# Where the last stage's weights are prepared: rounding and moments moved into the attention, GpSimd given two experts, shares computed before the weights' rests

## The chip, the cores and the metric

The kernel runs on one core of a Trainium2 chip. The metric is the device time of one execution in microseconds (us). A difference under about 0.2% (3.4 us here) can't be told from no change by such measurements.

## The reference

Four stages run on a tensor `h` of 4 batches of 750 tokens of 192 numbers: a token mixer, an attention with a mixture of experts (8 experts, 2 per token), a windowed attention of 12 heads with relative positions, and a second mixture of experts (8 experts, 1 per token). The change concerns the end of the third and the start of the fourth.

```
h = h + _L1_attn_ref(_layernorm(h), ...)
# _L1_ffn_ref(_layernorm(h), Ws, bs, W1, b1, W2, b2), x = normalised tokens
logits = xt @ Ws + bs
probs = softmax(logits); routes = argmax(probs); prob_max = max(probs)
h1 = gelu(einsum('td,edf->etf', xt, W1) + b1)      # 192 -> 768, per expert
y = einsum('etf,efd->etd', h1, W2) + b2            # 768 -> 192
out = y[routes] * prob_max
h = h + out
```

## The kernel before

Tokens lie in 24 blocks of 125 (`NT`), six per batch. Each stage is a block in which every engine has its own program, written out by hand, with semaphores between them; a stage begins when all engines have left the one before.

The windowed attention works on a batch in two halves of six heads. A half is 36 "words" (head u, query block c, x = 6(u-u0)+c): TensorE computes `scores(x+1)`, a further block of row scores (until x = 27) and `values(x-1)`; ScalarE takes the exponential twice per word (`Phi` rounded to fp32r and `PT` in fp32); VectorE forms the rest `Plo = PT - Phi` and the row maxima. `exp(x)` waits for `values(x-2)`, since there are two buffers. After the last word come the relative tables, the division, and the projection, whose six blocks VectorE adds to `h` (`update(0)` to `update(5)`).

The last stage (`moe` with `gated` false) routes tokens. VectorE normalises all 24 blocks into `xn` (L1367), TensorE turns them and computes logits, VectorE adds the router's bias (`lg`, L1437), ScalarE takes the exponential (L1303), VectorE finds the maximum and the expert (`oh`, `msk`), TensorE ranks tokens (L1131), VectorE turns ranks into positions, one-hot tables (`tile0`, `tile1`, `lane1`), TensorE multiplies them to lists (L1145), VectorE makes the gather list `take` and the scatter list `give`, and GpSimd gathers rows of 128 tokens. The list of experts per tile is `eid` (`owners()`). A loop over 31 tiles of 128 tokens follows, at about 4.7 us a tile. `keep_running(n)` issues n multiplications of the identity that compute nothing of use (L1083; each shows as two instructions); they stand where TensorE would otherwise wait.

The first weights W1 (192 x 768 per expert) are used as a rounded part plus a rest, for which each expert has four slots. `round_weights(e)` makes three copies to fp32r on ScalarE (L1266 to L1268), and `rest_of_weights(e)` two subtractions on VectorE (L1352, L1354). Experts 0 and 1 are loaded during the attention (`LOADED`), the others at the start of the last stage. Before, expert 0 is rounded behind the last words (L2619 to L2621) and its rests formed before the updates (L2932, L2934); expert 1 is rounded among the turned tokens, expert 2 before the exponential, the others behind it; the rests of expert 2 stand behind `msk`, those of 3 to 7 behind `give`. `divided()` divides the largest exponential by the sum; `part`, `tileP` (L1570) and TensorE's `probabilities()` (L1174) bring that share into the tiles' order. The first tile's product needs all rests (`s_wl`), the loop needs the shares.

The moments of `h` (mean, variance of each token) for batches 0 to 2 are formed in the last words; those of batch 3 in the last stage, among the normalisations (L1399, L1405).

Of the kernel before, what the change touches and what calls it, by code (L numbers as in the profile page):

```python
# [12 lines left out]
F32 = mybir.dt.float32  # L13
# [744 lines left out]
SOON = 2  # L758

LOADED = 2  # L760
# [41 lines left out]
def moe(nc, keep, A, h, ident, cfg, out, st=None, w1=None, wr=None, row=None, room=None, share=None, Y=None,  # L802
# [4 lines left out]
    with ctx:  # L807
# [41 lines left out]
        known = st is not None  # L849
        if not known:  # L850
            st = sb("st", [P, NT, 6])
# [90 lines left out]

        s_w1 = {} if cfg.gated else {e: sem(f"w1_{e}") for e in range(LOADED, NE)}
        s_wb, s_wh, s_wl, s_xo = (None if cfg.gated else sem(k) for k in ("wb", "wh", "wl", "xo"))
# [44 lines left out]
        def _(pool):  # L989
# [51 lines left out]

            pool.wait_ge(s_X, stored)
# [35 lines left out]
        def _(pe):  # L1078

            def keep_running(n):  # L1080

                for _ in range(n):
                    nc.tensor.matmul(spare[:, 0:128], ident[:], ident[:], start=True, stop=True)  # L1083

            ahead_of = dict(zip(("tiles", "rank", "list", "sums", "gather", "second", "shares"),
                                (16, 26, 60, 3, 28, 12, 0) if cfg.gated else (6, 18, 44, 3, 26, 8, 12)))
# [69 lines left out]
            def first_products(buf, e, order=FIRST):  # L1156
                half = cfg.cols // 2
                for g in range(2):
                    for x, (m, k) in enumerate(order):
                        if order is ROUNDED_FIRST and k == 1 and g == 0:  # L1160
                            pe.wait_ge(s_wl, NE)
# [17 lines left out]
            for j in range(2):  # L1179
# [4 lines left out]
                to_columns(j)  # L1184
            pe.wait_ge(s_xc, 1)
# [3 lines left out]
            else:  # L1189
                pe.wait_ge(s_wbr, 32)  # L1190
                pe.wait_ge(s_wh, NE)
# [8 lines left out]
            if not cfg.gated:  # L1200
                keep_running(ahead_of["shares"])
                probabilities()
                pe.wait_ge(s_w, 16 * (NE + 1))
# [37 lines left out]
        def _(act):  # L1241
# [20 lines left out]
            def round_weights(e):  # L1262

                if e >= LOADED:
                    act.wait_ge(s_w1[e], 32)
# [14 lines left out]

            for t in range(NT):
# [6 lines left out]
                else:  # L1288
                    if t == CH - 1:
                        act.wait_ge(s_wb, 16)  # L1290
                        nc.scalar.activation(bias_hi[:], bias_lo[:].bitcast(F32), ACT.Copy).then_inc(s_wb, 1)
                    if t % CH == CH - 1 and 0 < t // CH < SOON:
                        round_weights(t // CH)
                    if t == CH - 1:
                        roots(B - 1)

                        act.sem_inc(s_wh, 1)
                        nc.scalar.activation(warm[:], ident[0:1, 0:1], ACT.Exp)
            logits_out(NT // GROUP - 1)
            if not cfg.gated:  # L1300
                round_weights(SOON)
# [3 lines left out]
            if not cfg.gated:  # L1305
                for e in range(SOON + 1, NE):
                    round_weights(e)
# [38 lines left out]
        def _(dve):  # L1346
# [3 lines left out]
            def rest_of_weights(e):  # L1350
                dve.wait_ge(s_wh, e + 1)
# [44 lines left out]
            else:  # L1396
                def statistics(b):
# [1644 lines left out]
```

## Time and profile before

| | us |
|---|---|
| median of 3 runs | 1686.12 |
| lowest, highest | 1685.95, 1686.94 |
| profiled execution, its own time | 1683.9 |
| its span | 1682.0 |
| TensorE busy | 1586.4 (94%) |
| VectorE busy | 1172.5 (70%) |
| ScalarE busy | 983.9 (58%) |
| GpSimd busy | 415.2 (25%) |

The profiled execution took 1.9 us more than its span and 2.2 us less than the median of the runs. The attention's last half runs from about 1356 us (first exponential) to 1468.5 us (last update), the last stage's preparation from 1469.1 to 1525 us, and its loop to the end. Times of the rows are us from the span's start.

### The profile page before, as it was taken

How to read it: one execution, taken by the hardware profiler on the slowest of the kernel's cores; microseconds unless marked ns; L12 is line 12 of the kernel's file. 1: busy time of each engine (PE TensorE's matmuls, PEld its weight loads, DVE VectorE, ACT ScalarE, POOL GpSimd, SP SyncE). 2: the span in 40 equal slices, each digit the busy share in tenths (PEclk: the TensorE clock that was granted, in tenths of full speed). 3: DMA queues.
4: the chain of work that ended last, by engine and by line, in shares of the span. 5: the costliest groups of instructions: out<-in, count | busy, mean ns of one | idle time of the engine just before them, and what ended most of it. 6: DMA issues, size and time to landing. Idle time of an engine off the chain costs nothing. (4 is left out here: it accounts for less than half of the span.)

```text
span 1682.0 us, 32345 instructions
## 1 busy us (share of the span) xinstructions
PE 1586.4 (94%) x11573; PEld 1460.9 (87%) x11574; DVE 1172.5 (70%) x2224; ACT 983.9 (58%) x1775; POOL 415.2 (25%) x583
## 2 busy tenths in 40 slices
PE   5999999988999999999999999999999999889997
PEld 5788999977899888889898889888889988878996
DVE  4887555548776786786787677677677688575443
ACT  5542222225778678678677668767767857562331
POOL 4131566650102101210200310310300300014443
PEclk9999999988999999999999999999999999999999
DMA  9212111155101100100110110110110111091111
GB/s 271 72 47 85 52 56 58 56 131 142 45 11 40 45 11 24 61 11 11 44 40 10 30 46 20 30 46 20 30 46 11 39 50 38 23 299 52 60 59 29
DMA packets 61923, 94.73 MB, mean 56 GB/s; under 512 B 15644, under 2 KB 46511, under 8 KB 61422
## 3 DMA queue, kind: packets, MB, share of 16 engines
q1 hardware_dynamic: 52606, 72.92, 14.9%
q0 software_dynamic: 9200, 20.21, 4.2%
q8 instruction: 79, 1.29, 0.3%
q14 instruction: 38, 0.31, 0.1%
HBM read 72.58 MB, written 21.06 MB: 56 GB/s over the span
## 5 line engine op out<-in xcount | busy, mean ns | idle before, releaser
L2771 DVE TENSOR_REDUCE a_nmx<-a_M 125x1 f32<-125x752 f32 x256 | 240.6, 940 | 125.5 <-PE a_M L2239 125.0
L2593 ACT ACTIVATE a_Phi<-a_S 125x756 fp32r<-125x756 f32 x288 | 231.0, 802 | 159.3 <-PE a_O L2362 146.2
L2896 DVE TENSOR_TENSOR a_Plo<-a_PT,a_Phi 125x756 fp32r<-125x756 f32 x288 | 281.7, 978 | 51.7 <-ACT a_PT L2593 50.8
L2593 ACT ACTIVATE a_PT<-a_S 125x756 f32<-125x756 f32 x288 | 229.9, 798 | 0.0
L1989 POOL TENSOR_TENSOR a_qlo<-a_work,a_qhi 127x750 fp32r<-127x750 f32 x48 | 79.2, 1659 | 565.8 <-PE a_S L2343 494.7
L2343 PE MATMUL a_S<-a_qhi,a_khi 128*125 128x378 f32 x576 | 154.8, 350 | 10.5 <-issue 6.6
L2355 PE MATMUL a_O<-a_Phi,a_vhi 125*128 125x378 f32 x576 | 150.1, 342 | 1.3 <-ACT a_PT L2593 1.3
L2362 PE MATMUL a_O<-a_Plo,a_vhi 125*128 125x378 f32 x576 | 147.5, 337 | 1.0 <-DVE a_Plo L2896 0.9
L2343 PE MATMUL a_S<-a_qlo,a_khi 128*125 128x378 f32 x576 | 146.8, 336 | 0.0
L2343 PE MATMUL a_S<-a_qhi,a_klo 128*125 128x378 f32 x576 | 146.7, 336 | 0.0
L2358 PE MATMUL a_O<-a_Phi,a_vlo 125*64 125x378 f32 x576 | 146.4, 335 | 0.0
L1231 PE MATMUL m_psY<-m_w,m_hidT 128*128 x696 | 130.0, 330 | 2.8 <-DVE m_hidT L1588 2.8
L2239 PE MATMUL a_M<-a_khi,a_qhi 127*125 127x376 f32 x512 | 132.2, 339 | 0.2 <-DVE a_nmx L2771 0.2
L1231 PEld LDWEIGHTS m_psY<-m_w,m_hidT 128*128 128x128 f32 x696 | 114.4, 189 | 9.7 <-issue 9.7
L2343 PEld LDWEIGHTS a_S<-a_qhi,a_khi 128*125 128x125 f32 x576 | 98.4, 187 | 23.0 <-issue 15.9
L2362 PEld LDWEIGHTS a_O<-a_Plo,a_vhi 125*128 125x128 f32 x576 | 104.1, 189 | 14.5 <-DVE a_Plo L2896 4.3
L1315 ACT ACTIVATE m_xT<-m_psX 128x128 fp32r<-128x128 f32 x85 | 23.6, 277 | 153.1 <-PE m_psX L1153 153.1
L2355 PEld LDWEIGHTS a_O<-a_Phi,a_vhi 125*128 125x128 f32 x576 | 101.9, 190 | 11.2 <-issue 8.2
L1165 PE MATMUL m_psG<-m_w,m_xT 128*128 x540 | 109.2, 348 | 0.7 <-issue 0.6
L2015 POOL COPY a_by_column<-a_pairs 128x540 f32<-128x540 f32 x21 | 28.3, 1346 | 324.2 <-ACT a_pairs L2473 176.7
L2343 PEld LDWEIGHTS a_S<-a_qhi,a_klo 128*125 128x125 f32 x576 | 103.8, 187 | 0.0
L2343 PEld LDWEIGHTS a_S<-a_qlo,a_khi 128*125 128x125 f32 x576 | 103.7, 187 | 0.0
(463 smaller groups left out, 3273.1 us busy)
## 6 DMA issues: line engine op xcount, KB each, us to landing
a_qhi<-a_rdens SPq DMA_DIRECT2D x48, 187.5 KB, 3.3
a_wkv<-a_w4k SPq DMA_DIRECT2D x8, 768.0 KB, 5.2
a_wq<-a_w4q SPq DMA_DIRECT2D x8, 768.0 KB, 6.7
a_wkv<-a_w4v SPq DMA_DIRECT2D x8, 768.0 KB, 5.5
m_w<-in_m_w SPq DMA_DIRECT2D x8, 576.0 KB, 9.1
m_X<-m_xn SPq DMA_DIRECT2D x8, 504.0 KB
m_w<-in_m_w SPq DMA_DIRECT2D x8, 384.0 KB, 9.4
m_w_ahead<-in_m_w SPq DMA_DIRECT2D x8, 384.0 KB, 8.3
```

What stands on the lines that cost most here:

```text
L1165: last = nc.tensor.matmul(psG[buf][:, g, 0:half], tokens, w1[0:rows_, bass.ds(e, 1), k, g * half:(g + 1) * half].rearrange("d o f -> d (o ...
L1231: last = nc.tensor.matmul(psY[:, 0:E], hidT[:, k * 128:(k + 1) * 128], w2[:, bass.ds(here, 1), k, :].rearrange("f o e -> f (o e)"), start= ...
L1989: pool.tensor_tensor(qlo[0:ONE, u % HG % QLO, :], work[0:ONE, u % HG, 0:L], qhi[0:ONE, u % HG, :].bitcast(F32), ALU.subtract).then_inc(sg[ ...
L2015: pool.tensor_copy(to[:, pr, :, 0:GRID], rows[:, pr, 0:FULL, :])
L2239: last = nc.tensor.matmul(bank[0:P, a, 0:376], qhi[0:ONE, u % HG, c * P:(c + 1) * P], khi[0:ONE, u % HG, a * 374:a * 374 + 376], start=Tru ...
L2343: last = nc.tensor.matmul(psS[wd % 2][0:P, a, 0:HP], kk[:, u % HG, at], qq[:, PART[a]:PART[a] + HP], start=(x == 0), stop=(x == 2))
L2355: nc.tensor.matmul(psO[:, a, 0:HP], vhi[:, c, u % HG, :], Phi[:, wd % 2, at[a]], start=(c == 0), stop=False)
L2358: nc.tensor.matmul(psO[0:HD, a, 0:HP], vlo[:, c, u % HG, :], Phi[:, wd % 2, at[a]], start=False, stop=False)
L2362: last = nc.tensor.matmul(psO[:, a, 0:HP], vhi[:, c, u % HG, :], Plo[:, wd % 2, at[a]], start=False, stop=(c == CH - 1))
L2593: last = nc.scalar.activation(to[:, wd % 2, :].rearrange("p (a l) -> p a l", a=2), psS[wd % 2][0:P, :, 0:HP], ACT.Exp, scale=SCALE)
L2771: v.tensor_reduce(nmx[:, u % 2, c:c + 1], bank[0:P, :, 0:376], AX.XY, ALU.max, negate=True).then_inc(sg["max_ready"], 1)
L2896: v.tensor_tensor(Plo[:, wd % 2, :], PT[:, wd % 2, :], Phi[:, wd % 2, :].bitcast(F32), ALU.subtract).then_inc(sg["exp_rest"], 1)
```

## The change

- Experts 0 and 1 are rounded by ScalarE in the last batch's second half, one of six copies ahead of the exponentials of words 14 to 19 (`next_weights`), and their rests are formed by VectorE behind words 28, 30, 33 and 34 (`next_rests`).
- In the tables' memory the order is changed, so that both experts' slots are free by then.
- The moments of batch 3 move to the end of the attention: four `bn_stats` ahead of `update(5)`, two and the six aggregations behind it.
- GpSimd rounds the bias and experts 2 and 3, in seven copies behind the stores of zeros; ScalarE rounds experts 4 to 7.
- VectorE forms the rests of expert 2 before it takes the logits. Behind `msk` it divides; `owners()` moves behind `give`; `part` and `tileP` come before the rests of experts 3 to 7.
- TensorE computes the shares between the turning of the first and the second gathered tile; 26 spare multiplications stand before the first tile's product.

In VectorE's program, the last words of the attention stand like this before (`a_Plo` is the rest of a word, the last row but one the copy of turned sums, then the last word's rest and its output):

```order
L2860 TENSOR_SCALAR late<-late 125x18
L2896 TENSOR_TENSOR a_Plo<-a_PT,a_Phi 125x756 x2
L2881 COPY a_work<-a_turning 32x756
L2896 TENSOR_TENSOR a_Plo<-a_PT,a_Phi 125x756
L2873 COPY a_work<-a_O 96x378
```

and like this now:

```order
L2886 TENSOR_SCALAR late<-late 125x18
L2922 TENSOR_TENSOR a_Plo<-a_PT,a_Phi 125x756
L2860 SCALAR_TENSOR_TENSOR m_w_ahead<-m_w_ahead 128x768
L2922 TENSOR_TENSOR a_Plo<-a_PT,a_Phi 125x756
L2907 COPY a_work<-a_turning 32x756
L2860 SCALAR_TENSOR_TENSOR m_w_ahead<-m_w_ahead 64x768
L2922 TENSOR_TENSOR a_Plo<-a_PT,a_Phi 125x756
L2899 COPY a_work<-a_O 96x378
```

Two subtractions of weights now stand between the rests of the last three words.

VectorE behind the scatter list `give`, before:

```order
L1535 CAST m_give<-m_who 128x31
L1352 SCALAR_TENSOR_TENSOR m_w_ahead<-m_w_ahead 128x768
...
L1360 TENSOR_TENSOR m_xT<-m_psX,m_xT 128x128
L1361 TENSOR_TENSOR m_xT<-m_psX,m_xT 64x128
L1364 COPY m_hres<-m_xg 128x192
L1538 TENSOR_REDUCE m_lm<-m_lg 125x24
...
L1570 TENSOR_TENSOR m_tileP<-m_tile,m_part 125x2232
L1620 COPY m_prob<-m_psY 128x31
```

and now:

```order
L1533 CAST m_give<-m_who 128x31
L1510 TENSOR_TENSOR m_ecmp<-m_iots,m_cum 1x264
...
L1555 TENSOR_TENSOR m_tileP<-m_tile,m_part 125x2232
L1362 SCALAR_TENSOR_TENSOR m_w_ahead<-m_w_ahead 128x768
...
L1364 SCALAR_TENSOR_TENSOR m_w_ahead<-m_w_ahead 64x768
L1370 TENSOR_TENSOR m_xT<-m_psX,m_xT 128x128
L1371 TENSOR_TENSOR m_xT<-m_psX,m_xT 64x128
L1374 COPY m_hres<-m_xg 128x192
L1610 COPY m_prob<-m_psY 128x31
```

The owners and the shares have moved ahead of the ten subtractions of experts 3 to 7; the second tile's rests come last instead of `tileP`.

GpSimd ahead of the first gather, now (before, the gather followed the stores of zeros):

```order
L1022 DMA m_Y<-m_zero 128x192 x4
L1053 CAST m_bias_hi<-m_bias_lo 8x768
L1045 CAST m_w_ahead<-m_w_ahead 128x768
L1047 CAST m_w_ahead<-m_w_ahead 64x768
L1049 CAST m_w_ahead<-m_w_ahead 64x768
L1045 CAST m_w_ahead<-m_w_ahead 128x768
L1047 CAST m_w_ahead<-m_w_ahead 64x768
L1049 CAST m_w_ahead<-m_w_ahead 64x768
L1026 DMA m_xg<-m_X,m_take 128x384 x4
```

Seven copies have come between. The core of the diff:

```diff
+WEIGHTS_AT = 14
+RESTS_AT = (28, 30, 33, 34)
+BY_POOL = 2
...
+            def round_weights(n):
+                x = LOADED + n
+                pool.wait_ge(s_w1[x], 32)
+                pool.tensor_copy(w1[:, x, 0, :], w1[:, x, 1, :].bitcast(F32)).then_inc(s_wph, 1)
+                pool.wait_ge(s_wph, 3 * n + 1)
+                pool.tensor_copy(w1[64:128, x, 2, :], w1[0:64, x, 3, :].bitcast(F32)).then_inc(s_wph, 1)
...
+            if not cfg.gated:
+                pool.wait_ge(s_wb, 16)
+                pool.tensor_copy(bias_hi[:], bias_lo[:].bitcast(F32)).then_inc(s_wb, 1)
+                for n in range(BY_POOL):
+                    round_weights(n)
...
-                                (16, 26, 60, 3, 28, 12, 0) if cfg.gated else (6, 18, 44, 3, 26, 8, 12)))
+                                (16, 26, 60, 3, 28, 12, 0, 0) if cfg.gated else (6, 18, 44, 3, 26, 3, 2, 26)))
...
                 to_columns(j)
+                if j == 0 and not cfg.gated:
+                    keep_running(ahead_of["shares"])
+                    probabilities()
+            if not cfg.gated:
+                keep_running(ahead_of["rests"])
...
-            if not cfg.gated:
-                round_weights(SOON)
             act.wait_ge(s_ls, 1)
...
+                spread(B - 1)
...
-                for e in range(1, SOON):
-                    rest_of_weights(e)
+                rest_of_weights(LOADED)
...
                 v.tensor_copy(msk[:], oh[:, 0]).then_inc(s_m, 1)
-                rest_of_weights(SOON)
+                divided()
...
+                    if half == 1 and last_batch and WEIGHTS_AT <= x < WEIGHTS_AT + 3 * LOADED:
+                        next_weights(x - WEIGHTS_AT)
                     wait("scores_ready", wd + 1)
...
+                if new is None:
+                    for c in range(4):
+                        last_moments(c)
                 update(5)
+                if new is None:
+                    last_moments(4)
+                    last_moments(5)
+                    last_statistics()
...
+            def last_moments(c):
+
+                t = (B - 1) * CH + c
+                waiter(dve, B - 1)("h_updated", CH + c + 1)
+                v.bn_stats(st[:, t, :], h[:, t, :]).then_inc(s_v, 1)
+                link.n += 1
...
+                        if x in RESTS_AT:
+                            next_rests(RESTS_AT.index(x))
...
-                    dve.wait_ge(s_w11h, 1)
-                    v.scalar_tensor_tensor(w11[:, 0, 1, :], w11[:, 0, 1, :].bitcast(F32), 1.0,
-                                           w11[:, 0, 0, :].bitcast(F32), ALU.mult, ALU.subtract)
```

## Rows read from the trace of the kernel before

**Rows 1.** The chain that ended last, 1440 to 1542 us: start, us, what.
```profile
1480.16 1.67 PE m_psG L1094 x8
...
1485.18 0.85 PE m_psG L1094 x8
...
1488.56 0.84 ACT m_w_ahead L1267
...
1521.25 2.49 DVE m_tileP L1570
...
1525.26 0.66 PE m_psH L1217 x6
1525.92 1.74 PE m_psG L1165 x10
```

**Rows 2.** Timeline of ScalarE, then TensorE, in the words: start, us, engine, instruction, [idle before].
```profile
1396.72 0.80 ACT L2593 ACTIVATE a_Phi<-a_S 125x756 fp32r<-125x756 f32 x1
...
1399.33 0.59 PE L2343 MATMUL a_S<-a_qhi,a_khi 128*125 128x378 f32 x2 [0.19 <-issue]
```

**Rows 3.** Timeline, the attention's last word.
```profile
1445.32 0.94 DVE L2896 TENSOR_TENSOR a_Plo<-a_PT,a_Phi 125x756 fp32r<-125x756 f32 x1
...
1446.32 0.61 PE L2362 MATMUL a_O<-a_Plo,a_vhi 125*128 125x378 f32 x2 [0.19 <-DVE a_Plo L2896]
```

**Rows 4.** Timeline, the attention's end and the start of the last stage.
```profile
1468.19 0.35 DVE L2816 TENSOR_TENSOR h<-h,a_O 125x192 f32<-125x192 f32 x1 [0.62 <-PE a_O L2283]
...
1469.11 2.29 DVE L1367 TENSOR_SCALAR m_xn<-h,late 125x192 f32<-125x192 f32 x6 [0.56 <-PEq L1795]
...
1471.31 1.65 DVE L1399 BATCH_NORM_STATS2 m_st<-h 125x6 f32<-125x192 f32 x6
...
1472.25 2.29 POOL L1022 DMA_DIRECT2D m_Y<-m_zero  x4 [0.31 <-POOL m_xB L1018]
...
1474.63 0.49 DVE L1405 BATCH_NORM_AGGREGATE late<-m_st 125x2 f32<-125x6 f32 x6
```

**Rows 5.** GpSimd's groups over the span: line, shapes, count | busy us, mean ns | idle before.
```profile
L319 POOL TENSOR_TENSOR diag<-ident,rtc 64x768 f32<-64x768 f32 x1 | 1.5, 1463 | 6.0 <-DVE qku L640 6.0
...
L325 POOL MEMSET m_w<- 64x768 f32 x5 | 3.4, 732 | 11.3 <-DVEq L699 11.3
```

**Rows 6.** Timeline of GpSimd, then of VectorE at the same time.
```profile
1382.36 1.79 POOL L1989 TENSOR_TENSOR a_qlo<-a_work,a_qhi 127x750 fp32r<-127x750 f32 x1 [14.02 <-PE a_S L2343]
...
1383.54 1.41 DVE L2896 TENSOR_TENSOR a_Plo<-a_PT,a_Phi 125x756 fp32r<-125x756 f32 x1
```

**Rows 7.** Timeline, from the logits to the ranks.
```profile
1488.28 0.29 DVE L1437 TENSOR_TENSOR m_lg<-m_psH,m_row 125x128 f32<-125x128 f32 x1 [4.00 <-PE m_psY L1114]
...
1490.93 0.36 DVE L1448 TENSOR_TENSOR m_tmp<-m_lg,m_pe 125x192 f32<-125x192 f32 x1
...
1493.56 9.99 PE L1083 MATMUL m_psH<-ident 128*128 128x128 f32 x88
...
1494.41 0.34 DVE L1467 COPY m_tot<-m_psG 128x192 f32<-128x192 f32 x1
```

**Rows 8.** Timeline, from the lists to the first tile.
```profile
1505.75 0.41 DVE L1510 TENSOR_TENSOR m_ecmp<-m_iots,m_cum 1x264 f32<-1x264 f32 x1
...
1505.89 0.53 PE L1145 MATMUL m_psY<-m_tile,m_lane 125*128 125x62 bf16 x12 [0.31 <-DVE m_lane L1505]
...
1506.95 0.17 DVE L1519 COPY m_who<-m_psY 128x31 f32<-128x31 f32 x1
...
1508.88 0.95 DVE L1352 SCALAR_TENSOR_TENSOR m_w_ahead<-m_w_ahead 128x768 fp32r<-128x768 f32 x1
```

**Rows 9.** TensorE in single microseconds: stretch, length, busy, granted clock, DMA, GB/s.
```profile
1450.00:1451.00 1.00, 1.00 (x19) 0.50 0.10 6
...
1461.00:1462.00 1.00, 0.00 (x0) 1.00 0.00 0
```

**Rows 10.** DMA issues at 1492.4 to 1493.5 us: size, us to landing.
```profile
m_b<-in_m_b SPq DMA_DIRECT2D x1, 768.0 KB, 6.8
```

More of the change, by code:

```diff
@@ L1083, in keep_running @@
                     nc.tensor.matmul(spare[:, 0:128], ident[:], ident[:], start=True, stop=True)
-            ahead_of = dict(zip(("tiles", "rank", "list", "sums", "gather", "second", "shares"),
-                                (16, 26, 60, 3, 28, 12, 0) if cfg.gated else (6, 18, 44, 3, 26, 8, 12)))
+            ahead_of = dict(zip(("tiles", "rank", "list", "sums", "gather", "second", "shares", "rests"),
+                                (16, 26, 60, 3, 28, 12, 0, 0) if cfg.gated else (6, 18, 44, 3, 26, 3, 2, 26)))
             def turn_tiles(g):
@@ L1279, in logits_out @@
                 nc.scalar.activation(lgT[:, g, :], (psY, psX)[g % 2][:, 0:P], ACT.Copy).then_inc(s_lc, 1)
+            if not cfg.gated:
+                roots(B - 1)
+                nc.scalar.activation(warm[:], ident[0:1, 0:1], ACT.Exp)
             for t in range(NT):
@@ L1287, in _ @@
                         normalise(t + 5)
[L1288 to L1298, printed above, removed]
             logits_out(NT // GROUP - 1)
-            if not cfg.gated:
-                round_weights(SOON)
             act.wait_ge(s_ls, 1)
@@ L1305, in _ @@
             if not cfg.gated:
-                for e in range(SOON + 1, NE):
+                for e in range(LOADED + BY_POOL, NE):
                     round_weights(e)
@@ L1440, in _, with divided @@
             v.tensor_tensor(lg[:], lg[:], lm[:].unsqueeze(2).broadcast_to([P, NT, NE]), ALU.subtract).then_inc(s_ls, 1)
+            def divided():
+                link(v.tensor_reduce(lm[:], lg[:], AX.X, ALU.add))
+                link(v.reciprocal(lm[:], lm[:]))
+                for k in range(top):
+                    link(v.tensor_tensor(pe_[:, k, :], pe_[:, k, :], lm[:], ALU.mult))
             dve.wait_ge(s_ex, 1)
@@ L1514, in owners @@
                 v.tensor_copy(eid[:], eidf[:]).then_inc(s_eid, 1)
-            if not cfg.gated:
-                owners()
             dve.wait_ge(s_rank, 2)
@@ L1556, in _ @@
             else:
-                for e in range(SOON + 1, NE):
-                    if e == NE - 2:
-                        rest_of_tokens(0, 0)
-                    rest_of_weights(e)
-                rest_of_tokens(0, 1)
-                divided()
-            if not cfg.gated:
+                owners()
                 for x in range(PARTS):
@@ L1572, in _ @@
                                 ALU.mult).then_inc(s_part, 1)
+                for e in range(LOADED + 1, NE):
+                    if e == NE - 3:
+                        rest_of_tokens(0, 0)
+                    rest_of_weights(e)
+                rest_of_tokens(0, 1)
             v.sem_inc(s_h, 1)
```

75 lines of the change are left out of this document (34 added, 41 removed).

## The prediction

> **What bounds the kernel now.** I read the page first, then the chain that ended last, then the timelines of single engines where the change touches them. The page says that TensorE is busy for 94% of the span, and the loop over the last stage's tiles, some 4.7 us a tile, is untouched. What can change lies in two places. In the chain, the preparation of the last stage passes through pieces that the change moves: a rounding on ScalarE ahead of the exponential, `tileP` on VectorE, and then the first tile's transposes at 1525.26 [rows 1]. The other place is the attention's end, which the chain of that window doesn't list, so I read it from the timelines: which engine has room beside the words, and who waits for VectorE there. I count from T = 1469.1, the start of the last stage [rows 4].
>
> **The attention's words: ScalarE's six copies.** One copy takes 0.84 us [rows 1]. Ahead of word 14 ScalarE idles about as long, so I count the first one as free. Words 15 and 16 have turned sums ahead of them, and no idle time stands before word 16's exponential at 1396.72 [rows 2]: it starts two copies later, at 1398.4, and with two exponentials of 0.80, overlapping to 1.5 us together, ends at 1399.9. TensorE starts the scores of word 18 at 1399.33 [rows 2], and needs that buffer: 0.6 us lost. Copies 4 and 5 fall on words 17 and 18, which have idle time, copy 6 behind the output of a head at word 19, where by the same reckoning TensorE loses some 0.4. Sum +1.0; bounds 0 (TensorE's buffers cover it) and 2.5 (three copies in full, none hidden).
>
> **The words: VectorE's four subtractions.** One takes 0.95 us [rows 8]. Those behind words 28, 30 and 33 end before the exponential they could hold up, or before TensorE needs the rest; I take 0. The fourth stands directly ahead of the last word's rest, which began at 1445.32 without any idle time before it, and for whose end TensorE waited at 1446.32 [rows 3]. Nothing hides it: +0.9 (bounds 0.5 and 1.2). Everything behind it, to the projection, hangs on that word.
>
> **The moments.** Removed from VectorE ahead of the updates are the two subtractions of expert 0; that brings nothing, since the later updates wait for TensorE's projection anyway (idle 0.62 before the last) [rows 4]. Four `bn_stats` of 0.27 (1.65 for six) now precede the last update: 1.1 less the idle 0.62 is 0.5. Behind it stand two more (0.55) and the six aggregations (0.49) [rows 4]. Sum +1.5 (bounds 1.1 and 2.0). So the last stage starts 3.4 us later.
>
> **The last stage up to the logits.** Removed are six `bn_stats` and the aggregations, 2.1 us, and ScalarE's roundings of experts 1 and 2. Before, VectorE took the logits at 1488.28, T+19.2, and TensorE had been the last [rows 7]; Eight transposes took 1.67 in one part of this stretch and 0.85 in a later one [rows 1]: TensorE ran at half clock for a while. Without the gaps in `xn` I estimate it done at T+12.5 at full clock (six groups at 1.75: the 0.85 and as much again for logits) and at T+15.4 if two groups run at half speed; neither is on the path in my forecast. But now VectorE must first form the rests of expert 2, and waits for GpSimd. GpSimd is free at 1472.25 + 2.29, T+5.4 [rows 4]. Its copy of 768 elements isn't in the trace: a memset of 768 takes 0.73, a two-input operation of 768 takes 1.46, one of 750 takes 1.79 [rows 5, 6]. I take 1.45, the nearest in shape, and keep 0.73 and 1.8 as ends.
>
> What makes this more than four copies is that GpSimd and VectorE hold each other up. Where GpSimd worked from 1382.36 to 1384.15, VectorE's two-input rest took 1.41 instead of 0.94 [rows 3, 6]: it ended 0.8 us after GpSimd was done, as if begun then. So I go through the instructions, with 1.45 a copy: bias T+5.5 to 7.0; first copy of expert 2 to 8.5; VectorE, which has finished the 24 normalisations by then or at T+9.2 at the latest (four times 2.29 [rows 4]), holds it to 9.3 for the bias's rest; copies to 10.8 and 12.3. GpSimd goes straight on with expert 3, to 13.8, before VectorE's first subtraction can start; two subtractions end at 15.5; the logits are added; GpSimd's second copy of expert 3 ends at 17.0, the subtraction of the maximum follows, GpSimd's last ends at 18.75, and only then comes the comparison L1448. Before, that was at 1490.93, T+21.8 [rows 7]. The gain is 3.1, or 2.3 if GpSimd gets in between the two subtractions as well: −2.7. Bounds: −0.5 (copies of 1.8 us, every turn lost) and −5.4 (copies so short that TensorE is the last, at between the two ends above, with the 0.5 us that the rounding ahead of the exponential cost).
>
> The Trainium skill, *SBUF — State Buffer*, section "Who interferes with whom", has the rule behind this: VectorE and GpSimd share one pair of ports under an exclusive lock, a VectorE instruction with two SBUF inputs contends with a GpSimd one that reads SBUF, and the later one blocks fully; with one SBUF input it does not. By that rule the logits' addition, whose other input is in PSUM, is not held up, as I have it above; the row of the blocked subtraction agrees. The same skill, *GPSIMD Engine Reference*, section "Elementwise — side-by-side cycle accounting", gives 769 ns for 512 elements in a tight loop; my estimate from it for 768 is 1.15 us, and the same walk would give −4.9, a total of 1685.0. No run here shows it.
>
> **From the mask to the lists.** Behind `msk` two subtractions stood before the totals, which began at 1494.41, while TensorE had the ranks ready by 1493.56 plus its first spare's start, about 1493.7 [rows 7]. The division (three small operations of at most 0.36 each [rows 7]) ends about then: −0.7 (bounds −0.3 and −0.8). Moving the owners, 1505.75 to 1506.95, takes 1.2 from VectorE ahead of the lists [rows 8], but TensorE's last products of the list ended only at 1505.89 + 0.53, so −0.5 of it counts [rows 8] (bounds −0.3 and −0.7).
>
> **From `give` to the first tile.** Let G be the start of what follows `give`, 1508.88 before [rows 8]. VectorE worked without a gap from there to the end of `tileP`, 1521.25 + 2.49, 14.9 us, and TensorE's transposes of the first hidden tile came at G+16.4 [rows 1]. Now the division (0.9) is gone and the owners (1.2) come in: 15.2 us, of which the last 0.9 are the second tile's rests; the last rests of weights end at G+14.3. TensorE turns the second tile when VectorE has read the first, after owners, shares and two experts, at G+8.9, and then issues 26 spares: 88 instructions took 9.99 [rows 7], 52 take 5.9, so G+15.1. Then the first product, 1.74 [rows 1], and ScalarE's activation of 768 elements, about 0.8 as its copies, which before lay beside `tileP`: the transposes start at G+17.9. That is +1.6 (bounds +0.3, if the spares end sooner than the last rests and the first product waits only for its last terms; +2.0).
>
> **The sum** is +1.0 + 0.9 + 1.5 − 2.7 − 0.7 − 0.5 + 1.6 = +1.1 us. The profiled execution took 1683.9, and so the changed kernel's would take 1685.0; its own time lay 2.2 below the median of the runs, 1686.12, and on that scale the forecast is 1687.2. Less than 0.2% (3.4 us) is about what measurements of this kernel can't tell from no change: faster means below 1682.7, slower above 1689.5.
>
> **The rivals.**
> 1. *The two engines barely hold each other up, or GpSimd's copies are short.* Then the logits are taken at T+14 to 15, and the terms before the mask give −4.9 instead of −2.7: −1.1, that is 1685.0. For it: the memset of 0.73. Against: the two-input operations of 1.46 and more, and the blocked rest [rows 5, 6].
> 2. *Slower: TensorE's clock falls in the new gap before the 26 spares.* Once the shares are done (about G+6.2) and three spares with them (G+6.9), TensorE idles 2 us until the second tile. In an idle microsecond at 1461 the clock stayed full, but at 1450 to 1451, in the tables behind the last word's gap, it stood at half, 1.2 GHz [rows 9], and it did again in the last stage's transposes [rows 1]. If it falls here, the 5.9 us of spares, which stand ahead of the first product, cost between 0 and 5.9 more. With 3.2, the middle: 1690.4. It decides from a gap longer than the idle microsecond that did no harm; below that it costs nothing.
> 3. *Faster: what I put on the path is hidden.* TensorE's buffers cover the copies (0 instead of 1.0), the tail costs 0.3 instead of 1.6, and GpSimd is quick. The gain then meets another wait: the one-hot `lane1` also needs all rows of X stored, and the issue of `m_b`, which follows the last store, landed at 1492.4 + 6.8 = T+30.1 [rows 10], where `lane1` began at T+33.3. So at most 3.2 to about 6 us can come out of the stage up to there. With 5.6 (instead of the 2.7 and 0.7) the sum is 0 + 0.9 + 1.5 − 5.6 − 0.5 + 0.3 = −3.4; with VectorE's last subtraction hidden too it is −4.3: 1681.8.
>
> **How the numbers follow.** Forecast 0.46, rival 1 0.27, rival 2 0.15, rival 3 0.12. The likeliest gives 1687.2, with a range of its own from 1685.0 to 1689.5. The range for 8 in 10 leaves out most of rival 3 and the far half of rival 2: 1683.0 to 1690.5. Faster holds most of rival 3 and an edge of rival 1: 0.15. Slower holds most of rival 2 and the forecast's own upper edge (every turn at the port lost): 0.17. Same: 0.68.
>
> **What would show it.** In the profile after: word 16's exponential two copies late, and an idle time of TensorE of about 0.6 us before the scores of word 18; the last word's rest 0.9 later, with TensorE waiting for it; the last stage's start 3.4 us later; GpSimd's copies of about 1.45 us, and VectorE's subtractions and comparisons stretched beyond 0.95 and 0.36 where they overlap them; the totals started by TensorE's ranks; TensorE's spares ending after the last rests of weights. The forecast is wrong if GpSimd's copies take under 1 us or VectorE's instructions show their usual durations beside them, if TensorE shows half clock behind the second tile, or if the words' length in the last half hasn't changed.

## The result, and the profile after

The changed kernel took 1688.25 us in the median of 20 runs, the kernel before 1685.19 in 20 beside it: ratio 1.0016, 95% interval 1.0009 to 1.0023, so 2.7 us more (1.5 to 3.9). One run in each 20 took about 3070 us and is left out of the ratio. The forecast was 1687.2, called no measurable change because it lay within 0.2%; the time lies in its range and within that 0.2% too, though the interval says that the kernel did become a little slower. The sum held better than its terms did. The profiled execution took 1687.24 (span 1685.5, mean granted clock 0.978). Of its 3.5 us over the span of before, 1.4 are there at 1382 us, ahead of every changed place: TensorE's clock stood at 0.84 instead of 0.97 in the first 150 us. So I compare stages, not points in time.

T is the start of the last stage, now 1472.9. All times are us of a run's own span.

**The words.** Timelines of the kernel after: ScalarE at word 16 with the copies around it, TensorE before word 18's scores; then VectorE's last subtraction and TensorE's last products. Columns as in [rows 2, 3].

```profile
1399.01 0.84 ACT L2445 ACTIVATE m_w_ahead<-m_w_ahead 64x768 fp32r<-64x768 f32 x1
1399.76 0.78 ACT L2594 ACTIVATE a_Phi<-a_S 125x756 fp32r<-125x756 f32 x1
...
1401.37 0.58 PE L2333 MATMUL a_S<-a_qhi,a_khi 128*125 128x378 f32 x2 [0.55 <-ACT a_PT L2594]
...
1447.69 0.95 DVE L2860 SCALAR_TENSOR_TENSOR m_w_ahead<-m_w_ahead 64x768 fp32r<-64x768 f32 x1
1448.57 0.93 DVE L2922 TENSOR_TENSOR a_Plo<-a_PT,a_Phi 125x756 fp32r<-125x756 f32 x1
...
1449.55 0.61 PE L2352 MATMUL a_O<-a_Plo,a_vhi 125*128 125x378 f32 x2 [1.05 <-DVE a_Plo L2922]
```

Word 16's exponential began at 1396.72 before [rows 2]; this run was 1.39 later ahead of the first copy, and the exponential is another 1.65 late. TensorE waits 0.55, and its wait ahead of the last products has grown from 0.19 to 1.05. From GpSimd's rest at 1382 us ([rows 6]; 1383.76 here) to the last word's rest it took 62.96 before and takes 64.81.

**To the last stage.** VectorE's moments, then SyncE's first issue of the stage, which is T.

```profile
1469.93 1.13 DVE L2866 BATCH_NORM_STATS2 a_PT<-h 125x6 f32<-125x192 f32 x4
1470.98 0.34 DVE L2813 TENSOR_TENSOR h<-h,a_O 125x192 f32<-125x192 f32 x1
1471.23 0.61 DVE L2866 BATCH_NORM_STATS2 a_PT<-h 125x6 f32<-125x192 f32 x2
1471.88 0.51 DVE L2873 BATCH_NORM_AGGREGATE late<-a_PT 125x2 f32<-125x6 f32 x6
...
1472.91 0.36 SPq L956 DMA_DIRECT2D m_wr<-in_m_wr  x1
```

The last update has no idle time ahead of it any more (0.62 in [rows 4]), and T follows it by 1.93 instead of 0.88.

**The last stage up to the totals.** VectorE and GpSimd side by side.

```profile
1479.49 4.33 DVE L1377 TENSOR_SCALAR m_xn<-h,late 125x192 f32<-125x192 f32 x6
1483.75 0.94 DVE L1419 TENSOR_TENSOR m_bias_lo<-m_bias_lo,m_bias_hi 8x768 fp32r<-8x768 f32 x1
...
1486.87 0.29 DVE L1431 TENSOR_TENSOR m_lg<-m_psH,m_row 125x128 f32<-125x128 f32 x1 [0.45 <-PE m_psY L1128]
...
1489.03 0.36 DVE L1448 TENSOR_TENSOR m_tmp<-m_lg,m_pe 125x192 f32<-125x192 f32 x1
...
1491.92 0.36 DVE L1467 COPY m_tot<-m_psG 128x192 f32<-128x192 f32 x1 [0.26 <-PE m_psG L1146]
```

```profile
1480.34 0.82 POOL L1045 CAST m_w_ahead<-m_w_ahead 128x768 fp32r<-128x768 f32 x1 [1.10 <-DMA m_w_ahead<-in_m_w]
...
1482.89 0.82 POOL L1045 CAST m_w_ahead<-m_w_ahead 128x768 fp32r<-128x768 f32 x1
1483.78 3.34 POOL L1047 CAST m_w_ahead<-m_w_ahead 64x768 fp32r<-64x768 f32 x1
```

A copy on GpSimd takes 0.82 us. The two engines do hold each other up: six normalisations took 4.33 instead of 2.29 [rows 4] beside four casts, and one cast 3.34 beside VectorE's subtractions. But in this profile TensorE is the last here (0.45), so the comparison comes at T+16.1 instead of T+21.8 [rows 7].

**From the lists to the loop.** Timelines of VectorE, GpSimd and TensorE.

```profile
1503.99 0.19 DVE L1517 COPY m_who<-m_psY 128x31 f32<-128x31 f32 x1 [0.63 <-PE m_psY L1159]
...
1506.10 1.17 POOL L1026 DMA_INDIRECT m_xg<-m_X,m_take  x1 [18.10 <-DVE m_give L1533]
...
1513.94 0.33 PE L1166 MATMUL m_psX<-ident,m_xg 128*128 128x128 f32 x1 [4.09 <-DMA m_xg<-m_X,m_take]
...
1517.53 0.42 PE L1166 MATMUL m_psX<-ident,m_xg 128*128 128x128 f32 x1
...
1517.96 6.28 PE L1097 MATMUL m_psH<-ident 128*128 128x128 f32 x52
1523.99 0.95 PE L1179 MATMUL m_psG<-m_w_ahead,m_xT 128*128 x4
...
1527.07 0.87 PE L1235 MATMUL m_psH<-ident,m_hid 128*128 128x128 f32 x6 [0.84 <-ACT m_hid L1341]
```

`give` is written 32.95 us into the stage instead of 39.72, 6.8 sooner. The first gather is issued 2.9 us sooner by the clock than before and used at 1513.94, 0.85 later than before (1513.09). The 52 matmuls are the 26 spares; VectorE's last rest for the weights had ended at 1521.1. Two windows from 1510 to 1512, of before and then of after (length; busy us and count of TensorE, its weight loads, VectorE, ScalarE, GpSimd; granted clock; share of the DMA engines; GB/s), show why the gather was late:

```profile
1510.00:1512.00 2.00, 2.00 (x20) 2.00 (x19) 2.00 (x3) 0.00 (x0) 1.70 (x2) 1.00 0.31 83
```

```profile
1510.00:1512.00 2.00, 0.00 (x0) 0.00 (x0) 2.00 (x3) 0.00 (x0) 1.89 (x1) 1.00 1.03 401
```

The loads of the second weights, `w2` (768 x 192 per expert), are the last of a string that begins with the stage. SyncE's issues of them, before and then now:

```profile
1495.09 4.93 SPq L980 DMA_DIRECT2D m_w<-in_m_w  x8
```

```profile
1498.10 4.58 SPq L980 DMA_DIRECT2D m_w<-in_m_w  x8
```

That is 26.0 us into the stage before and 25.2 now, while the gather's issue moved from 40.0 to 33.2. The engines are still full when the lists are ready; e1 tests whether that is these loads.

**The loop.** Something I had not looked for: starts of the transposes of hidden tiles, three in a row around the place where the loop turns, before and after.

```profile
1567.95 0.82 PE L1217 MATMUL m_psH<-ident,m_hid 128*128 128x128 f32 x6
1572.77 0.82 PE L1217 MATMUL m_psH<-ident,m_hid 128*128 128x128 f32 x6
1577.47 0.82 PE L1217 MATMUL m_psH<-ident,m_hid 128*128 128x128 f32 x6
```

```profile
1570.39 0.82 PE L1235 MATMUL m_psH<-ident,m_hid 128*128 128x128 f32 x6
1575.34 0.82 PE L1235 MATMUL m_psH<-ident,m_hid 128*128 128x128 f32 x6
1580.05 0.82 PE L1235 MATMUL m_psH<-ident,m_hid 128*128 128x128 f32 x6
```

A plain tile takes 4.70 in both; the tile at the turn took 4.82 and takes 4.95. There are six such turns behind the first, and the first takes 5.45 instead of 5.22; from the second hidden tile to the last it is 138.25 us instead of 137.27. Another 0.4 lie at the very end, behind the issue of the last scatter (8.69 us to the end of the span instead of 8.27). No line of the diff touches the loop.

### The profile page after: what moved, and what is told of

It reads as the page before. It is cut to its first block and busy times, and to the rows that moved or that the text cites. A ratio compares the mean times of both kernels' runs of the same rounds, so it can differ in the third digit from the quotient of the medians.

```text
span 1685.5 us, 32390 instructions
## 1 busy us (share of the span) xinstructions
PE 1588.0 (94%) x11595; PEld 1462.4 (87%) x11596; DVE 1175.9 (70%) x2224; ACT 979.6 (58%) x1768; POOL 426.0 (25%) x590
## 3 DMA queue, kind: packets, MB, share of 16 engines
q1 hardware_dynamic: 52606, 72.92, 14.8%
## 5 line engine op out<-in xcount | busy, mean ns | idle before, releaser
L2333 PE MATMUL a_S<-a_qhi,a_khi 128*125 128x378 f32 x576 | 155.1, 350 | 11.3 <-issue 6.5
L1249 PEld LDWEIGHTS m_psY<-m_w,m_hidT 128*128 128x128 f32 x696 | 114.4, 189 | 10.2 <-issue 10.2
```

Source lines behind the costliest of these rows:

```text
L1249: last = nc.tensor.matmul(psY[:, 0:E], hidT[:, k * 128:(k + 1) * 128], w2[:, bass.ds(here, 1), k, :].rearrange("f o e -> f (o e)"), start= ...
L2333: last = nc.tensor.matmul(psS[wd % 2][0:P, a, 0:HP], kk[:, u % HG, at], qq[:, PART[a]:PART[a] + HP], start=(x == 0), stop=(x == 2))
```

## The experiments

Each was timed in five rounds beside the kernel before. The table gives stages of the profiled execution (us): the words (GpSimd's rest near 1382 to the last word's rest), from there to T, from T to `give`, to the first gathered tile on TensorE, to the first hidden tile's transposes, and from the second hidden tile to the end of the span; then the ratio of times to the kernel before, with its interval.

```
                     words  to T   give   tile   hidden  rest    ratio
before               62.96  23.75  39.72  44.02  56.03   152.34
after                64.81  24.34  32.95  41.03  54.16   153.74  1.0016 [1.0009, 1.0023]
e1 half of w2 later  64.87  25.14  32.18  36.92  51.05   153.66  1.0001 [0.9991, 1.0012]
e2 no 26 spares      64.85  26.32  33.02  40.42  51.50   153.72  1.0008 [0.9996, 1.0019]
e3 moments in stage  64.85  25.53  39.68  44.40  58.02   152.74  1.0020 [1.0010, 1.0030]
e4 before, w2 later  63.01  23.93  41.03  45.23  60.33   152.38  1.0022 [1.0006, 1.0038]
e5 words' places     63.39  26.94  33.05  40.86  54.70   153.68  1.0012 [0.9999, 1.0024]
e6 tail as before    64.83  25.14  33.03  37.55  53.74   153.77  1.0013 [1.0004, 1.0023]
e7 e5 and e6         63.37  24.52  33.80  38.64  53.12   153.72  1.0000 [0.9988, 1.0011]
e8 e3, root too      64.85  25.55  37.66  42.27  57.63   152.80  1.0021 [1.0010, 1.0032]
e9 12 memsets        64.87  25.36  32.69  40.29  54.60   152.65  1.0002 [0.9988, 1.0015]
e10 unused st        64.87  28.47  33.05  40.81  54.75   153.71  1.0019 [1.0004, 1.0034]
e11 best without e9  63.41  26.97  32.98  38.50  50.46   153.70  0.9991 [0.9978, 1.0004]
e12 e11 and e9       63.35  26.32  33.09  37.62  50.56   152.58  0.9977 [0.9966, 0.9988]
```

The words, the gap to the end and, mostly, `give` repeat to 0.1 us; the stretch to T doesn't, and below I say what that leaves open.

### e1: do the loads hold up the gather?

```
 for e in range(NE):
+    if e == NE // 2 and not cfg.gated:
+        sp.wait_ge(s_in[RING - 1], 16)
     sp.dma_start(w2[:, e], ...)
```

SyncE holds back the loads of `w2` for experts 4 to 7 until the fourth gather has landed.

> The changed kernel, but SyncE issues the loads of w2 for experts 4 to 7 only when the fourth gather has landed, so that the gathers meet empty transfer queues. Theory Q (the first gather of the changed kernel waits behind the string of loads, which began 3.8 us later with the last stage and still needs its time): the gather lands about 4 us after its issue instead of 7.8, TensorE's idle 4.09 us before the first gathered tile goes to about 0.5, the second tile is turned as soon as VectorE has read the first (its stall of 0.51 gone), the 26 spares follow, and the first product starts 2.4 us sooner than in the changed kernel: total about -2.4 us, if the late half of w2 (2.3 MB, some 6 us of transfer) is there for the second product. Rival L (the gather is slow by itself, for instance because its descriptors are written while VectorE holds the shared port): it lands 7 to 8 us after its issue as before, total 0. Rival W: w2 comes too late, TensorE waits for it before the first second product, total +1 to +3.

TensorE's timeline:

```profile
1513.82 0.33 PE L1168 MATMUL m_psX<-ident,m_xg 128*128 128x128 f32 x1 [0.75 <-DMA m_xg<-m_X,m_take]
...
1518.39 0.30 PE L1168 MATMUL m_psX<-ident,m_xg 128*128 128x128 f32 x1 [1.89 <-DVE m_xT L1373]
...
1527.68 0.32 PE L1168 MATMUL m_psX<-ident,m_xg 128*128 128x128 f32 x1 [1.31 <-DMA m_w<-in_m_w]
```

Theory Q holds: TensorE takes the tile 4.5 us after the gather's issue (1509.32) instead of 7.8, and its wait fell from 4.09 to 0.75. The second tile then waits for VectorE, and w2 came a little late: some of rival W is in it as well. The ratio fell from 1.0016 to 1.0001, 2.5 us. To the first hidden tile the stage is 3.1 shorter, but not all of that comes from the loads: `give` itself is 0.8 sooner, because VectorE could take the logits 12.97 us into the stage instead of 13.96:

```profile
1489.87 0.29 DVE L1433 TENSOR_TENSOR m_lg<-m_psH,m_row 125x128 f32<-125x128 f32 x1 [0.21 <-PE m_psY L1130]
```

TensorE was the last there in both profiles, at a granted clock of 1.00 from T to the logits in e1 and of 0.88 in the profile after; the loads of `w2` are issued later than that, so the edit has no part in it. Behind `give` it is 18.87 instead of 21.21: 2.3 us, close to the 2.4 expected. The later runs agree: those that hold back half of `w2` (e6, e7, e11, e12) used the first gather 4.3 to 5.3 us after its issue, and those of the changed kernel's order that don't (e2, e5, e9, e10) 7.2 to 7.6.

### e2: are the 26 spares in the way?

```
-    ... (6, 18, 44, 3, 26, 3, 2, 26)))
+    ... (6, 18, 44, 3, 26, 3, 2, 0)))
```

> The changed kernel without the 26 spare transposes ahead of the first product. Theory S (they stand in the way: they start with the late second tile and end 2.9 us after VectorE's last rests): the first product's rounded terms run at once, its other terms start with the last rests at about 15 us after give, and the first hidden tile is turned 2.5 to 3 us sooner: total about -2.8. Rival C (they keep the clock up, and without them the first products and transposes run at half clock): the first product takes some 3.5 us instead of 1.9 and the next stretch too, total between -1 and +1.

```profile
1520.18 0.68 PE L1179 MATMUL m_psG<-m_w_ahead,m_xT 128*128 x1 [2.43 <-DVE m_w_ahead L1364]
...
1523.85 1.54 PE L1235 MATMUL m_psH<-ident,m_hid 128*128 128x128 f32 x6 [0.64 <-ACT m_hid L1341]
```

Both theories have their share. The first hidden tile came 2.7 us sooner in the stage, as S says. But TensorE idled 2.43, worked at half clock behind it (those transposes take 1.54 instead of 0.87), and the second hidden tile came 5.93 behind the first instead of 4.69: 1.2 given back, as C says. By the ratio 1.3 us are left, within the intervals.

### e3 and e8: the moments back in the last stage

```
-                for c in range(4): last_moments(c)
                 update(5)
-                last_moments(4); last_moments(5); last_statistics()
...
-                spread(B - 1)
                 for b in range(B):
+                    if b == 1: statistics(B - 1)
+                    if b == 2: spread(B - 1)
```

> The changed kernel with the last batch's moments back in the last stage, as in the kernel before (six bn_stats between the first and second batch of the normalisations, six bn_aggr behind the second). Theory Q (the string of loads, which begins with the last stage, sets when the first gather lands): the last stage starts 1.4 us sooner, the string ends 1.4 sooner and so does the gather, while the 2.1 us that VectorE needs more ahead of the lists are hidden behind it: total -1.4, and the idle time before the first gathered tile falls from 4.09 to about 2. Rival V (VectorE's chain to the lists sets it): the lists come 0.7 later, total +0.7, and the idle time before the gathered tile stays at 4.

This measured something else than I meant. ScalarE's root now stands first in its order, and it waited for the moments; TensorE waited for ScalarE's copies:

```profile
1480.11 0.21 ACT L1265 ACTIVATE late<-late 125x6 f32<-125x6 f32 x1 [20.89 <-DVE late L1420]
```

```profile
1482.23 1.87 PE L1110 MATMUL m_psG<-ident,m_xn 125*96 125x125 f32 x8 [6.05 <-ACT m_xnT L1293]
```

e8 also moved the root and its warming activation back behind the sixth tile.

> The changed kernel with the moments in the last stage and ScalarE's root behind its sixth tile again, as in the kernel before (in the third experiment the root stood first in ScalarE's order and held up all its copies until the moments were done). Theory Q (string of loads): the stage starts 1.4 us sooner behind the last word (1 us of noise by TensorE's clock in the tables), the lists come 1 to 2 us later in the stage, and the gather lands as far into the stage as in the changed kernel, 41 us: stage to the first hidden tile 54.2, total -1.4. Rival V (VectorE's chain): the lists come 2.1 us later in the stage and the first hidden tile too, 56.3, total +0.7.

`give` came 4.7 us later in the stage than in the changed kernel, more than V's 2.1, and the first hidden tile 3.5 later; the ratio is 1.0021. All of the 4.7 is there at the logits already (18.67 us into the stage instead of 13.96). With the moments among them, the third batch's normalisations fell on GpSimd's casts:

```profile
1479.89 5.48 DVE L1379 TENSOR_SCALAR m_xn<-h,late 125x192 f32<-125x192 f32 x6
```

That is 3.7 more than the second batch's 1.83, and TensorE then was the last at the logits (2.36). Q's use of it fails: with lists that late the loads are no longer the limit. So by the stages the moments are worth their 1.4 us ahead of the last one; the ratios of e8 and of the changed kernel are too close to tell. What e3 and e8 gave by accident is the last column: 152.7 and 152.8.

### e4: the kernel before with the later w2

> The kernel before with the same later half of w2 as the first experiment. Theory Q: here the lists came when the string of loads was already ending (give 39.8 us into the stage, the gather landing 4.0 us after its issue, hidden behind VectorE's rests), so there is nothing to gain: total 0, within 0.7. If the gather was slowed here too, it would land in 3 us or less, and still gain nothing, since VectorE works without a gap up to tileP. Rival W: the late half of w2 delays the first second product: +1 or more.

The gathers come as before, and then TensorE waits for w2:

```profile
1528.59 0.32 PE L1154 MATMUL m_psX<-ident,m_xg 128*128 128x128 f32 x1 [2.32 <-DMA m_w<-in_m_w]
```

Rival W: +3.7 by the ratio. Of the 4.3 us in the stage, 1.3 are in `give` already, and they come from the logits, for which VectorE waited longer than before (4.00 in [rows 7]):

```profile
1489.06 0.29 DVE L1439 TENSOR_TENSOR m_lg<-m_psH,m_row 125x128 f32<-125x128 f32 x1 [5.31 <-PE m_psY L1116]
```

That is 20.53 us into the stage instead of 19.21, at a granted clock of 0.75 instead of 0.82 from T to there; the edit acts only on loads that are issued behind the logits, so this is TensorE's clock and not the edit. The other 3.0 lie behind `give`. The same edit gains where the lists are early and costs where they are late, so what it buys is not the loads' order by itself.

### e5: other places in the words

```
-WEIGHTS_AT = 14                    # words 14 to 19
-RESTS_AT = (28, 30, 33, 34)
+WEIGHTS_AT = (14, 17, 18, 19, 20, 23)
+RESTS_AT = (27, 28, 30, 33)
```

> The changed kernel with the six copies on ScalarE in the last half's words 14, 17, 18, 19, 20 and 23 instead of 14 to 19 (where the kernel before shows ScalarE idle 0.8 to 1.4 us ahead of the exponential or of the output), and the four subtractions on VectorE behind words 27, 28, 30 and 33 instead of 28, 30, 33 and 34. Theory P (the 1.85 us that the words are longer in every trace of the changed kernel's kind are the copies of words 15 and 16, which stack on the turned sums, and the subtraction ahead of the last rest): from GpSimd's rest at 1382 us to the last word's rest 63.0 to 63.2 us as in the kernel before instead of 64.85, TensorE's wait for the last rest 0.2 instead of 1.05, total -1.8. Rival M (work on ScalarE and VectorE costs wherever it stands, since the words are bound by these two as well): 64.2 or more, total -0.5 or less.

The words took 63.39, and TensorE's last wait was 0.19 again: P, for 1.42 of the 1.85 us. The other 0.4 is in words 13 to 24, so it is what the six copies still cost in these places. The ratio fell by 0.0004 only, within its interval; in this profile the stretch to T was 26.94, the longest but two, and took it back.

### e6 and e7: the order behind `give`

In e6 `owners()` is followed by the rests, then shares and `tileP`; TensorE's `probabilities()` stands behind the first product again, without the 26 spares, and SyncE waits for `s_in[0]`, the first gather. e7 is e6 with e5.

> The changed kernel, with the late half of w2 behind the first gather instead of the fourth (the first experiment showed a wait of 1.31 us for it), and behind give the order of the kernel before: owners, the rests of weights and of the two tiles, then shares and tileP; on TensorE second tile, first product, 12 spares, shares; the 26 spares are gone. Theory O (with tileP ahead, VectorE reaches the last rests only at 14.8 us after give, and what follows takes 2.8 us): last rests at about 11.5, tileP ends at about 15.2, its products 1.7, first hidden tile turned at about 17 us after give and 50 us into the stage instead of 54.2: total -4 against the changed kernel. Rival: with VectorE in that order, tileP and its 24 products bound just as late (17.7 or more), total -3 or less; and if w2 still comes late it shows as a wait of TensorE before the first hidden tile.

> The two former experiments in one kernel. If their gains lie in different stages and nothing else becomes the bound, they add: about -5.8 against the changed kernel, -3 against the kernel before. If the time of the stage is set by the string of loads (which starts with the stage), the gain is that of the words and of the first experiment alone, -4.2 against the changed kernel.

```profile
1518.33 0.33 PE L1168 MATMUL m_psX<-ident,m_xg 128*128 128x128 f32 x1 [4.09 <-DMA m_xg<-m_X,m_take]
```

That is e7's second tile. I had let the late half of w2 go when the first gather had landed, so it ran into the second, and TensorE waited 4.09 us again, one tile later (4.93 in e6, whose first hidden tile came only 0.4 sooner than the changed kernel's, and not 4). Theory O wasn't tested by it. The ratio of e7 is that of the kernel before, 1.0000, with the shorter words (63.37) and the stage 1.0 shorter than the changed kernel's.

### e9 and e10: why does the loop turn more slowly?

```
+                for _ in range(12):                    # e9, VectorE, ahead of the loop
+                    link(v.memset(lm[0:1, 0:1], 0.0))
...
+            st = sb("st", [P, NT, 6])                  # e10, unused
```

> In the loop over the tiles every fourth tile, where the loop turns, takes 4.94 us in all traces of the changed kernel's kind and 4.82 in the kernel before and in the two kernels with the moments in the last stage (the first turn 5.44 against 5.22): 1.1 us over the run. At the turn VectorE's first operation comes 0.13 us later. This is the changed kernel with 12 memsets of one element on VectorE, ahead of the loop, where it idles 5.6 us; its loop then begins as many instructions (118) into its part of the program as in the kernels that turn in 4.82. Theory I (the place of VectorE's loop in its instruction stream sets the cost of its jump): 4.82, total -1.1. Rival A (the place of tiles in SBUF, since the kernels that turn fast also have a tile st): 4.94, total 0.

> The changed kernel with a tile st of 576 bytes per partition in the last stage that nothing uses, so that the tiles behind it lie where they lay in the kernel before. Theory I (instruction stream): the turn of the loop stays at 4.94 us, total 0. Rival A (place of tiles in SBUF): 4.82, total -1.1.

Hidden tiles around a turn in e9, then in e10:

```profile
1571.81 0.82 PE L1235 MATMUL m_psH<-ident,m_hid 128*128 128x128 f32 x6
1576.64 0.82 PE L1235 MATMUL m_psH<-ident,m_hid 128*128 128x128 f32 x6
```

```profile
1578.21 0.82 PE L1237 MATMUL m_psH<-ident,m_hid 128*128 128x128 f32 x6
1583.16 0.82 PE L1237 MATMUL m_psH<-ident,m_hid 128*128 128x128 f32 x6
```

4.83 with the memsets, 4.95 with the tile: the instructions ahead of the loop set it, not the tiles' places. The first turn went from 5.45 to 5.07, and the stretch to the end from 153.7 to 152.65; by the ratio the kernel gained 2.4 us, with an interval that holds 1.1. The traces show 118 VectorE instructions between T and the loop before, 116 in e3, e8, e9 and e12, and 104 in the kernels that turn slowly (the expectation counts 118 for e9 where the trace shows 116). From the program's start to the loop they show 2044 in all kernels but e9 and e12, so it is not that number.

### e11 and e12: what the runs point to

e11 is e5, SyncE's wait on `s_in[1]`, the second gather, and 22 spares instead of 26. e12 adds the 12 memsets.

> The changed kernel with copies and subtractions in the words' other places (fifth experiment), the late half of w2 behind the second gather (behind the first, it delayed the second gather, and TensorE waited 4.09 us for that), and 22 spares instead of 26, in the changed kernel's order behind give. Theory Q: both gathers land before VectorE can use them, no wait for w2; first hidden tile 49.7 us into the stage instead of 54.2, the words 1.4 shorter, total -5 against the changed kernel by the traces, and -1.5 to -2.5 against the kernel before, less what TensorE's clock in the tables adds. Rival: the second gather waits again, or w2 comes late, and the stage is 51 us or longer.

> The kernel of the eleventh experiment (words' other places, late half of w2 behind the second gather, 22 spares) with the 12 memsets of the ninth. Theory: the gains lie in different places and add. Every fourth tile 4.82 instead of 4.94, and the first turn 5.1 instead of 5.4: -1.1 us against the eleventh, about -2.7 us against the kernel before (ratio 0.998 to 0.9985), the first hidden tile 50.5 us into the stage. Rival: the memsets, or the link between them, hold up the first hidden tile's copy by up to 1 us, and the gain is nothing.

```profile
1512.08 0.33 PE L1168 MATMUL m_psX<-ident,m_xg 128*128 128x128 f32 x1 [0.55 <-DMA m_xg<-m_X,m_take]
...
1516.86 0.30 PE L1168 MATMUL m_psX<-ident,m_xg 128*128 128x128 f32 x1 [2.09 <-DVE m_xT L1373]
...
1525.02 0.87 PE L1237 MATMUL m_psH<-ident,m_hid 128*128 128x128 f32 x6 [0.84 <-ACT m_hid L1343]
```

In e11 the stage took 50.46 us to the first hidden tile, 3.7 less than in the changed kernel, and the ratio fell to 0.9991, with an interval that holds no change. In e12 neither the gather nor w2 holds up TensorE much, and VectorE's work of 14.5 us behind `give`, up to the last rests, is the limit again. The memsets took 1.33 in VectorE's idle time. e12 is faster than the kernel before: 1682.04 us in the median against 1685.55 beside it, 0.9977 [0.9966, 0.9988], 2.0 to 5.7 us less. The changed kernel was not run beside it, but its interval (1.0009 to 1.0023) lies wholly above. Between e11 and e12, as between the changed kernel and e9, the ratio differs by 2.4 us, more than the 1.1 that the traces show; the intervals hold both.

## Why the prediction was right, and where its terms were not

The forecast was no measurable change, +1.1; the runs say +2.7 (1.5 to 3.9). The time was right, and the mechanism in part only. The prediction had named signs that it would be wrong, and two of them are there: GpSimd's copies took under 1 us (0.82), and TensorE shows half clock around the second tile (0.50 from 1516 to 1518). Step by step, forecast and then measured:

- *ScalarE's copies* +1.0: +1.0 (words 13 to 24 took 0.97 longer), with the two places, 0.55 instead of 0.6 before word 18. e5 shows that the copies' places made 0.6 of it.
- *The fourth subtraction* +0.9: +0.88. Right; e5 took it away.
- *The moments* +1.5: +1.4 in two profiles whose tables took 10.2 as before (e1, e6: 25.14 against 23.75), +1.6 in a third (e9, 25.36).
- *Up to the mask* −2.7: **−5.7**. This step was mis-sized. I took 1.45 us for a cast, from two-input operations; it takes 0.82, near the memset I had as the lower end. The mutual blocking is real, but it fell on the normalisations and on GpSimd's own casts, while TensorE set the time. That is rival 1, and more than the bound of −5.4. How firmly TensorE is the limit differs: in e5, e6, e7, e9, e10 and e11 VectorE does not wait for it at the logits, and takes them 13.3 to 14.8 us into the stage; in e6 it waited 0.73 for a GpSimd copy, and its subtraction took 1.55. And the 19.21 before is itself a value of TensorE's clock (20.53 in e4), so −5.7 is uncertain by a microsecond or so.
- *Behind the mask and the owners* −0.7 and −0.5: −0.6 (2.89 instead of 3.48) and −0.5 (12.07 from totals to `who` instead of 12.54).
- *From `give` to the first hidden tile* +1.6: **+4.9** (21.21 instead of 16.31, from `give`). I had looked at the engines and not asked whether the gather would still land in 4 us. Its issue moved 6.8 us forward in the stage, into transfers whose start hangs on the stage's start. e1 shows 2.3 us of it; the other 0.8 of its 3.1 is TensorE's clock ahead of the logits. With both gathers early and four spares fewer (e11, e12) 17.5 are left, +1.2. The forecast's own terms don't quite add up here: 15.1, 1.74 and 0.8 are 17.6 and not 17.9, +1.3 instead of +1.6. Rival 3 had the right kind of limit, a string of transfers, at the wrong place (`lane1`, which didn't wait).
- *The loop* 0: **+1.4**. The prediction had no term for it. 1.0 of it are the turns, which e9 took away (137.17 from the second hidden tile to the last). The other 0.4 stand behind the issue of the last scatter, in every run of the changed kernel and its variants (8.6 to 8.7, against 8.27 before and 8.29 in e4); what causes them is open.

These measured terms add up to +2.8. Errors of 3.0 in one direction and 4.7 in the other left the sum 1.7 off. That the time fell into the range was luck to that extent: with the late gather and the loop foreseen and the casts not, or the other way round, it would have been off by 3 us or more.

Rival 2 happened in small (its price of 3.2, called the middle of 0 and 5.9, should have been 2.95). TensorE idled, behind the late gather rather than behind the shares; its clock stood at 0.50 from 1516.0 to 1517.5, and the 26 spares took 6.28 instead of 5.9.

The Trainium skill, *SBUF — State Buffer*, section "Who interferes with whom", also says that a `tensor_scalar` on VectorE can enter a two-port mode and then contends with GpSimd. I had used only that section's sentence on single inputs, and without its condition: it holds outside those modes. The six normalisations of one input are `tensor_scalar`, and at 4.33 instead of 2.29 the trace agrees with the part that I had passed over.

**Open.** From the last word's rest to T the two profiles without the change show 23.75 and 23.93, the others 24.3 to 28.5. Moments explain 1.4, but e3 and e8 have none there and still took 25.5. Most of the differences go with TensorE's clock in the tables' products, which took 8.6 us (three profiles), 10.2 (five), 11.3 to 11.7 (five) or 13.0 (e10) for the same work. e12 is an exception: its tables took 8.6 and the stretch 26.3, and there the half clock fell on the projection (its first 12 products took 3.70 us instead of 2.19). Windows of e10 in that stretch, columns as above:

```profile
1456.00:1458.00 2.00, 2.00 (x36) 2.00 (x34) 0.00 (x0) 0.58 (x1) 0.00 (x0) 0.50 0.08 11
1458.00:1460.00 2.00, 2.00 (x35) 2.00 (x33) 0.27 (x1) 0.58 (x1) 0.00 (x0) 0.50 0.05 3
```

Whether the change makes that more frequent, one profile for each kernel can't tell. Nor do the runs say what makes the turn cheap at one place in the stream and dear at another.

## What to carry to other kernels

When a change brings a step forward in a stage, read the DMA share at the step's new time, not at its old one: a transfer's 4 us are good only for the load of the queues it was seen in, and a string of loads that starts with the stage does not move forward with the lists. Extra work on a secondary engine belongs where its timeline shows idle time ahead of the instruction that another waits for; moved by one to four words it cost 1.4 us less. A cast that is moved to another engine can still hold up the first: look at what the two do at the same time. And compare a loop's period before and after, even if no line of it was changed.

## What was new of the hardware

- A conversion of 768 elements to the rounded format takes GpSimd 0.82 us alone, about what ScalarE takes (0.84); beside VectorE's two-input operations one took 3.34.
- The same loop turned in 4.82 or 4.95 us by the instructions that stood ahead of it on VectorE; 12 memsets outside it took 1.1 us out of the loop's trace.
- An indirect gather that was used 4.0 to 4.6 us after its issue where the loads were over or held back (5.3 in e11) took 7.2 to 7.8 behind them, with the DMA engines at a share of 1.03 (0.31 at the same time before).
